# Three seams of a fused recurrent, attention and expert layer: loads moved among stores, additions moved into the experts, an earlier first wait of the experts

## The reference

```
x = x + gated_scan(layernorm(x))        # hidden/gate projection 128 -> 2*192, log-space scan over the
                                        # 256 tokens of a sequence, projection 192 -> 128
z = layernorm(x)                        # the "base" of the second layer
h = layernorm(z)*g1 + b1;  q, k, v = h@Wq, h@Wk, h@Wv      # 16 heads of 8 channels
z = z + softmax(q k^T / sqrt(8)) v @ Wo
m = layernorm(z)*g2 + b2;  probs = softmax(m @ Wg)         # 8 experts, each token takes the top 2
z = z + sum_k weight_k * expert_k(m)    # expert: 128 -> 512, gelu (tanh form), 512 -> 128, with biases
out = x + z
```

## Time and profile before

| | |
|---|---|
| median of 3 runs | 1054.08 us (1046.05 to 1059.02) |
| profiled execution | 1052.99 us, span 1051.1 us |
| mean PEclk | 0.873 |
| busy | PE 787.5 us, PEld 484.2, DVE 804.0, ACT 583.0, POOL 529.8 |
| third stage ends (last DVE parts) | 206.3 us |
| first row maximum on DVE | 211.48 us |
| last output projection of the attention added | 688.6 us |
| last table of the routing written | 721.3 us |
| first split on DVE | 730.29 us |
| last expert block's rows stored | 964 us |

### The profile page before, as it was taken

How to read it: one execution, slowest core, us unless ns; L and a number is a source line. 1 busy time by engine, 2 the same in 40 slices (tenths; PEclk the granted TensorE clock), 3 DMA queues, 4 the chain that set the end, 5 groups by cost and what they waited for, 6 DMA issues and landing times.

```text
span 1051.1 us, 25392 instructions
## 1 busy us (share of the span) xinstructions
PE 787.5 (75%) x8366; PEld 484.2 (46%) x8367; DVE 804.0 (76%) x1600; ACT 583.0 (55%) x1198; POOL 529.8 (50%) x669
## 2 busy tenths in 40 slices
PE   3777746588998989898879888834999999994000
PEld 2455534323444444343424344322888888884000
DVE  7788779686886798989887989156888888888512
ACT  6745358625765678787646778722555555552000
POOL 9600089600225372625118587843777146665775
PEclk9999889955987899999968999966999999998555
DMA  7820013411211111211011221102555445553432
GB/s 188 306 102 1 1 41 127 168 47 42 58 42 41 38 52 53 66 36 39 18 32 42 60 65 55 34 5 56 134 132 137 103 116 131 129 128 100 122 82 73
DMA packets 132071, 84.16 MB, mean 80 GB/s; under 512 B 54520, under 2 KB 117628, under 8 KB 131982
## 3 DMA queue, kind: packets, MB, share of 16 engines
q1 hardware_dynamic: 123790, 66.20, 21.8%
q0 software_dynamic: 8192, 16.79, 6.0%
HBM read 30.25 MB, written 41.94 MB: 69 GB/s over the span
## 4 chain that ended last, share of the span: by engine, by line
PE 60%; DVE 10%; POOL 9%; ACT 8%; issue 8%; DMA 1%; ACTq 0%; SPq 0%; POOLq 0%; DVEq 0%
PE bank L1337 57%; ACT arena L855 5%; POOL HT L757 3%; POOL Z L757 3%; DVE arena L1036 2%; PE bank L1341 1%; POOL rr L497 1%; PE bank L1517 1%; DVE arena L1100 1%; POOL xh L501 1%; DVE Z L1020 1%; DVE mom L955 1%; ACT arena L765 1%; DVE Z L1027 1%; ACT Z L806 0%
## 5 line engine op out<-in xcount | busy, mean ns | idle before, releaser
L1100 DVE TENSOR_REDUCE arena<-bank 128x2 f32<-128x512 f32 x512 | 329.8, 685 | 77.5 <-PE bank L1337 75.2
L855 ACT ACTIVATE arena<-bank 128x512 f32<-128x512 f32 x512 | 285.9, 594 | 136.0 <-PE bank L1337 134.8
L1337 PE MATMUL bank<-QK 31*128 31x256 f16 (+1 forms) x2048 | 183.7, 295 | 56.4 <-ACT arena L855 31.3
L1337 PE MATMUL bank<-w2p,QK 128*128 x1280 | 216.5, 246 | 1.4 <-DVE arena L1300 1.4
L928 ACT ACTIVATE arena<-bank,b1s 128x256 f32<-128x256 f32 x320 | 125.3, 475 | 102.4 <-PE bank L1337 99.9
L1337 PE MATMUL bank<-arena,w1h 128*128 128x256 f16 x640 | 166.3, 277 | 10.4 <-DMA arena<-expert_in 8.9
L689 POOL DMA_INDIRECT expert_in<-HT,idx x128 | 133.2, 1041 | 71.7 <-issue 35.9
L1337 PE MATMUL bank<-arena,VA 128*32 128x256 f32 x2048 | 151.7, 418 | 0.7 <-ACT arena L855 0.7
L1337 PEld LDWEIGHTS bank<-QK 32*128 32x128 f16 (+1 forms) x2048 | 52.0, 94 | 191.0 <-ACT arena L855 145.6
L1337 PEld LDWEIGHTS bank<-w2p,QK 128*128 128x128 f16 x1280 | 124.0, 98 | 10.7 <-issue 1.7
L1295 DVE TENSOR_TENSOR QK<-arena,QK 128x1024 f16<-128x1024 f32 x80 | 98.0, 1225 | 2.7
(11 more groups left out here) (158 smaller groups left out, 1152.5 us busy)
## 6 DMA issues: line engine op xcount, KB each, us to landing
QK<-qk_parts SPq DMA_DIRECT2D x96, 128.0 KB, 2.7
expert_in<-arena SPq DMA_DIRECT2D x40, 256.0 KB, 3.2
expert_out<-arena SPq DMA_DIRECT2D x80, 128.0 KB
qk_parts<-arena SPq DMA_DIRECT2D x16, 512.0 KB, 2.8
X<-x SPq DMA_DIRECT2D x8, 512.0 KB, 5.9
wst<-w SPq DMA_DIRECT2D x16, 256.0 KB, 2.8
out<-arena SPq DMA_DIRECT2D x16, 256.0 KB, 2.6
expert_in<-HT,idx POOLq DMA_INDIRECT x128
```

What stands on the lines that cost most here:

```text
L855: nc.scalar.activation(PT[t % 8], bank[3 + t % 2][:, :], ACT.Exp, scale=DH ** -0.5)\
L1100: V.tensor_reduce(nmax[n % 2][:, :, 4 * j + g], bank[u % 3][:, :].rearrange("p (q t) -> p q t", q=2), AX.X, ALU.max, negate=True).then_inc ...
L1337: return nc.tensor.matmul(dst, lhsT, rhs, start=start, stop=stop)
```

## The change

Three edits.

(a) SP's `load_qk(0)`, `(1)` and `(2)` no longer stand behind all 16 stores of q and k but behind the fourth, fifth and sixth. For it ACT now waits, before `max_evac(0)`, until all 16 stores have landed.

(b) `base(4)` to `base(7)` no longer stand between `lo5(7)` and the scatters of part 1 but among these, behind the two scatters of the 12th, 16th, 20th and 24th tile of the part.

(c) SP begins to load expert blocks after the last logits (`lg_done` at 32) instead of after the second table; ACT and PE begin on the first table. PE waits besides for the second reading of the counts (`cnt_read` at 2), since its first `up`s write bank 4. ACT and PE wait for the second table between two loops, at block 32, so their loop is now broken in two as SP's was.

```diff
--- before.py
+++ after.py
@@ -414,12 +414,6 @@
             for s in range(4):
                 sp.dma_start(QK[s][31::32, :, :, :].rearrange("j g c t -> j (g c t)"), const_sel).then_inc(edge_in, 16)
 
-            for i in range(NG):
-                sp.wait_ge(hi_ready, i + 1)
-                sp.wait_ge(lo_ready, i + 1)
-                sp.dma_start(hl_dram[2 * i:2 * i + 2].rearrange("b p c t -> p b (c t)"),
-                             hl[i % 2].rearrange("p b c t -> p b (c t)")).then_inc(hl_out[i % 2], 16)
-
             def load_qk(n):
                 k = n // 2
                 sp.wait_ge(hl_out[k % 2], 16 * (k // 2 + 1))
@@ -431,13 +425,18 @@
                     sp.dma_start(QK[n % 4][r::4, :, :, :], hl_dram[n, :, q:k + 1:k - q, :]
                                  .rearrange("(m g) c t -> m g c t", g=4)).then_inc(qk_in[n % 4], 16)
 
+            for i in range(NG):
+                sp.wait_ge(hi_ready, i + 1)
+                sp.wait_ge(lo_ready, i + 1)
+                sp.dma_start(hl_dram[2 * i:2 * i + 2].rearrange("b p c t -> p b (c t)"),
+                             hl[i % 2].rearrange("p b c t -> p b (c t)")).then_inc(hl_out[i % 2], 16)
+                if 3 <= i < 6:
+                    load_qk(i - 3)
+
             def load_max(n):
                 sp.wait_ge(nmt_ready, n + 1)
                 sp.dma_start(QK[n % 4][31::32, :, 0, :], nmt[n % 2])\
                   .then_inc(nmt_in[n % 4], 16)
-
-            for n in range(3):
-                load_qk(n)
 
             def load_weight(k):
                 if k >= 2:
@@ -473,7 +472,7 @@
                     load_block(b + 7, (q + 3) % 4)
                 store_block(b, q % 2)
 
-            sp.wait_ge(tab_ready, 2)
+            sp.wait_ge(lg_done, 2 * NO)
             sp.wait_ge(scattered[0], 32 * HN)
             for b in range(7):
                 if b >= 4:
@@ -732,8 +731,6 @@
             pool.wait_ge(norm_last, 1)
             nc.gpsimd.tensor_tensor(rr[1][:, 0, :], vv[1][:, 0, :], mhalf[:, 0, :], ALU.pow).then_inc(rs_last, 1)
             lo5(LAST)
-            for j in range(OCT0[1], NO):
-                base(j)
             pool.wait_ge(mh_ready, NO)
             pool.wait_ge(idx_ready, 2)
             for n in range(HN, NT):
@@ -742,6 +739,8 @@
                     if ahead >= 0:
                         pool.wait_ge(down_done, ahead * (HBLK - 10) // (2 * (NT - HN) - 8) + 1)
                     scatter(n, k)
+                if (n - HN) % 4 == 3 and 8 <= n - HN < 24:
+                    base(OCT0[1] + (n - HN - 8) // 4)
 
             pool.wait_ge(base_ready, NO)
             pool.wait_ge(scattered[0], 32 * HN)
@@ -884,6 +883,8 @@
                 n = TILE0[part + 1] - TILE0[part]
                 nc.scalar.activation(w_2[:, 0:n], dif[:, 0:n], ACT.Exp).then_inc(exp6, 1)
 
+            for s in range(2):
+                act.wait_ge(hl_out[s], 16 * NG // 2)
             max_evac(0)
             for b in range(NB + 1):
                 for c in range(16):
@@ -918,7 +919,7 @@
             exp_gate(1)
 
 
-            act.wait_ge(tab_ready, 2)
+            act.wait_ge(tab_ready, 1)
 
             def gelu(b, s):
                 e = act.value_load(blke[0:1, bass.ds(b, 1)], min_val=0, max_val=NE - 1)
@@ -934,7 +935,7 @@
                 if exists(b + 2):
                     gelu(b + 2, q % 2)
 
-            blocks(act, -2, experts)
+            blocks(act, -2, experts, second_part=lambda: act.wait_ge(tab_ready, 2))
 
 
         @block.vector
@@ -1601,7 +1602,8 @@
             counts(1, bank[4][:, 0:2 * NE])
 
 
-            pe.wait_ge(tab_ready, 2)
+            pe.wait_ge(tab_ready, 1)
+            pe.wait_ge(cnt_read, 2)
             pe.wait_ge(wsplit, 4 * NE)
 
             pe.wait_ge(b2_ready, 1)
@@ -1678,7 +1680,7 @@
                         for k in range(4):
                             pe.reg_mov(carried[k], known[4 + k])
 
-            blocks(pe, -3, experts)
+            blocks(pe, -3, experts, second_part=lambda: pe.wait_ge(tab_ready, 2))
 
 
 # ---- launch: one core; numpy lays the arrays out ----
```

## The result

On one chip the changed kernel took **1032.79 us** (median of 4 runs, 1027.75 to 1042.31) and the kernel before 1050.97 (4 runs): ratio **0.987, 95% interval 0.982 to 0.992**, 8.5 to 18.8 us less with 13.7 in the middle. The ratio is taken from fast runs alone and is not the quotient of the two medians, which would be 0.983 and 18.2 us. The profiled execution took 1042.31 us, 10.7 less than that of before; its span is 1040.5 us against 1051.1. Where the 10.6 us between the spans come from, read from the starts of the same instructions in both traces.

The account below looks back on a forecast made before the run. Bounds: the loads' place in SP's list, then DVE's routing held by POOL's additions, then PE in the experts. 5.1 + 15.6 - 2.5 - 1.0 - 1.2 = 16.0 us less; counted from the median 1054.08, 1038 us, range 1028 to 1047.

Parts of the forecast that it names:

- (a): Third stage's end to the attention: with loads amid the stores, DVE's first maximum comes at 206.4 instead of 211.48, 5.1 us gained.
- second seam: Routing to experts: shorter routing and PE's earlier start bring the first split to 714.7 instead of 730.29, 15.6 us gained.
- The additions in the experts: Expert blocks: the four moved POOL additions delay DVE, and 2.5 us of it reach PE; bounds 0 and 9.8.
- the rival of full length: Expert blocks: the additions cost DVE 9.8 us instead of 2.5, late scatters 2 instead of 1; time 1046, chance 0.18.
- Late scatters: POOL's longer list in the experts: the part lands 2 to 7 us late for SP, costing 1.0 us (bounds 0 and 4).
- Broken loop: Between two expert loops at block 32: a second loop exit costs 1.2 us, upper bound 2.5.
- The clock through the first seam: Third stage to attention: with PE's 7.3 us gap gone the clock stays up, 8.7 us more gained; 1029, chance 0.13.
- Routing not shortened: Second routing: its four long instructions were slow for another reason, so 8.2 us gained instead of 15.6; 1045, chance 0.04.
- POOL starved: Experts: DVE keeps POOL from SBUF, an addition takes 8.6 us, SP stands and PE runs dry; 1061, chance 0.03.

Follow-up runs that it names:

- the first group's chip: Chip on which each part alone and the whole change ran against the kernel before, which took 1113.96 us there; the whole change had ratio 0.9958.
- the kernel with pieces: The whole change with its four additions cut into 32 of one 128 x 128 tile, one behind each of 32 scatters; ratio 1.0056.
- the kernel with fillers: Matmuls with unused results added before and through the lead stretch and the attention's first 20 steps, on the last addition behind the scatters; ratio 0.9927.
- one a block: The last addition behind the scatters, but its eight pieces one at a time, each behind the end of one of blocks 32 to 39; ratio 0.9807.
- the last addition behind the scatters: Three additions in the attention, but with the last octet's eight pieces back to back behind the last scatter; ratio 0.9854.
- three additions in the attention: The whole change with the additions of octets 4 to 6 moved into the attention, the last in eight pieces behind eight scatters; 1027.96 us, ratio 0.9802.

## Why the prediction was right, point by point

The forecast was 16.0 us less; measured were 13.7 (8.5 to 18.8) by the runs and 10.6 by the profiles. The spans' difference of 5.4 us from the forecast is the additions (5.9 - 2.5 = 3.4), the attention (3.5), the second seam (0.8) and the 0.4 before the route, less 2.2 for two terms that came to nothing, 0.4 at the first seam and 0.1 at the end. So some luck is in it: two costs that did not appear pay for most of what the additions cost beyond the forecast. Luck of the chip too: on the first group's chip the same change had 0.9958. And the time, 1032.79 for a forecast of 1038, is 5 us lower though the gain was smaller, since the forecast counts from a median before of 1054.08, which the fourth run brought to 1050.97.

- **(a), 5.1 us: right, 5.5.** DVE follows its own last part. The loads amid the stores cost nothing that can be seen. ACT's new wait cost nothing: its first evacuation started at 216.86, released by PE. The profile shows only 1.95 us of the gain at the last exponential, and the clock explains most of the 3.5 that are missing: between the first and the last exponential TensorE stood at 1.2 GHz for 105.5 us after and for 96.9 before. At the paces of the earlier trace rows, 1.10 and 0.80 us per exponential, 8.6 us at the low level cost an estimated 8.6 x 0.30 / 1.10 = 2.3 us; 1.2 stay open. The moved loads don't seem to cause it: the low stretches add up to 96.9 and 79.3 us in two profiles of the kernel before, and to 105.5, 94.9, 61.6 and 84.1 in the four with the loads moved on chips of this pace. Alone the loads gave 0.9922, 8.7 us (4.3 to 12.9), which holds 5.1.
- **Second seam, 15.6 us: right, 14.8.** The route got 7.3 us shorter for the 7.4 forecast. What failed by 0.8 is "PE may start when the counts are read": it started 1.10 us later, and the first split waited for ACT. From the first `up` to the first split it took 5.85 us, for 5.84 forecast; ACT's table load, which the rows cited there don't show, is in it with 1.28 us.
- **The additions in the experts, 2.5 us: the term that was mis-sized.** They cost 5.9 us by the profiles' blocks and 5.2 by the kernel without them. The estimate let the subtraction wait and left the cast open. It is the cast that waits, and not for an average piece of the addition: the two engines had fallen into step, so the cast, begun at 761.65, meets the whole of the addition begun at 761.72, and the two later ones likewise: (1.97 + 3.00 + 2.99 + 2.98) - 4 x 0.69 = 8.2 us held. The working had 1.8 us per addition, 7.2 in all, so the delay itself was not far off. What failed is how much of it DVE's spare time absorbs. The working took off 0.34 us of slack in each of 4.3 blocks and "about one more" for the buffers, which leaves 1.4 us or less; the 2.5 that stand in the sum lie above that without a reason given, and still too low. PE loses at once what the buffers ahead of it don't cover (the four GELU intervals exceed 2.74 by 0.56, 1.51, 1.50 and 1.47, 5.0 us in all), and slack in later blocks doesn't give it back. The wait itself was foreseen, and the bounds 0 and 9.8 hold; the rival of full length (9.8) was too dear here, and nearly right on the first group's chip (8.0, with cast and subtraction held in turn).
- **Late scatters, 1.0 us: nothing.** POOL's additions took 2.35 to 2.61 us, the last scatter began at 811.2 and SP asked for the part at 816.48, since the blocks themselves had become later.
- **Broken loop, 1.2 us: nothing** that the GELUs' intervals show (3.12 and 2.78 us at block 32).
- **Rivals.** The clock through the first seam: false, and with TensorE kept busy still false. Routing not shortened: false. POOL starved: false for this change (2.35 to 2.61 us per addition); its end, SP standing, came with 32 pieces, 1.0056, by a longer list.

VectorE and POOL together: by the Trainium skill (SBUF — State Buffer, Who interferes with whom) a cast can enter a 2-port mode, and whichever of it and a GpSimd instruction issues first has the shared pair for the whole instruction. The trace agrees that one waits for the other's whole instruction, 3.00 us against 0.69; with it the term would have been four casts held. Which of the two goes first can't be read from the records' starts, and POOL's are rough: with the cast 0.07 us ahead it is the cast that waits beside an addition (761.65 and 761.72), and the piece that waits in the kernel with pieces (712.05 and 712.12: cast 0.69, piece 0.93 for 0.46). It also agrees that `tensor_reduce` never contends (0.60 us each beside an addition in the attention, though reading PSUM; and 0.42 at 706.13 in the kernel before, reading SBUF beside an addition) and that a subtraction with two SBUF inputs is held by any GpSimd instruction that reads SBUF (2.27 against 1.23).

The clock: with 6.00 of 6.00 us busy in 206 to 212 us the clock went to 0.50. The Trainium skill (TensorE: Matmul & The Clock Gate, What's actually happening) has the busy state at full clock and the idle one at half; in 212 to 232 us of the kernel with fillers, 10.00 of 10.00 us busy twice at 0.50, the trace does not agree.

## What to carry to other kernels

Work that is moved off a seam must be priced by what it holds where it lands: ask which of the neighbour's instructions read or write SBUF on both sides, and whether the two engines fall into step, since then it isn't the average that meets but each time the worst. Such additions showed no cost beside instructions that read PSUM and write next to nothing, and cost 5 to 8 us beside SBUF-to-SBUF casts and subtractions. Cutting a long instruction into small ones frees the neighbour only if something stands between them (8 pieces back to back held a cast for 3.05 us, one a block none). It costs the own engine time (32 pieces 22.7 us, four additions 9.7), so its own deadline must have room.

## What the runs showed that was not expected

- **Chips differ by stage.** The kernel before took 1048 us on one chip and 1108 to 1114 on two others. Expert blocks 10 to 31 took 60.0 to 61.0 us there and 66.3 to 67.2 here with no long addition among them, with TensorE at full clock in both stretches shown. On the slower chip TensorE was busy 61.46 of 66.90 us and on the faster 58.94 of 60.50; of its weight loads' idle time in that stretch 10.2 us in 21 gaps are put down to "issue", against 2.8 in 5. The additions cost 7 to 8 us there instead of 5.2, and they met casts and subtractions in turn instead of casts alone. Why the weight loads come late was not looked into. The two stretches, slower chip first (the last addition behind the scatters; three additions in the attention):

```profile
772.60:839.50 66.90, 61.46 (x626) 51.23 (x624) 52.96 (x64) 33.00 (x84) 40.71 (x39) 1.00 0.46 121
```
```profile
733.00:793.50 60.50, 58.94 (x633) 52.46 (x631) 54.23 (x64) 32.93 (x84) 50.14 (x46) 1.00 0.50 131
```

- **A small addition has a floor.** 128x128 took 0.44 to 0.47 us alone, where an eighth of 2.36 is 0.3. Begun while DVE's cast or subtraction ran, a piece mostly ended 0.30 to 0.32 us behind it, and took 0.60 to 1.48 by that. The other way round, a cast that a long POOL instruction holds ends 0.55 or 0.56 us behind it and a subtraction 1.07 to 1.09, in the four kernels that have them.
- **A scatter waits for DVE too.** Alone it takes 0.96 us. Where it begins while DVE's cast or subtraction runs, it ends 0.82 to 0.84 us behind the end of that instruction: 33 of the 64 scatters in the kernel without additions, 23 behind a cast and 10 behind a subtraction, whatever they took in all, up to 1.67 us. In the kernel with pieces such scatters end 0.82 to 0.95 us behind, so the piece ahead doesn't stretch them itself; it moves their start into DVE's subtraction. From the kernel without additions, POOL, then DVE:

```profile
740.84 1.67 POOL L688 DMA_INDIRECT expert_in<-HT,idx  x1 [0.30 <-issue]
```
```profile
740.45 1.23 DVE L1294 TENSOR_TENSOR QK<-arena,QK 128x1024 f16<-128x1024 f32 x1
```
